# Scatters of a routed expert stage on GpSimd, with and without a small memset between them

## The chip, the cores and the metric

The kernel runs on one core of a Trainium2 chip. The metric is the device time of one execution in microseconds (us), median of several runs; lower is better. The engines are TensorE (PE in the profile), VectorE (DVE), ScalarE (ACT), GpSimd (POOL) and SyncE (SP). SP here only issues DMAs. POOL issues indirect DMAs, whose rows go to, or come from, places that a list of numbers names.

## What is computed

A small vision tower: 64 images become 4096 tokens of 256 numbers, then come an attention layer, a routed expert layer with 7 experts, a second attention layer and, last, a second expert layer. The change lies in that last layer. Cut to what matters, it is:

```
combine = _route(xf, router_weight, router_bias)      # top 4 of 16 experts, by groups
out = jnp.zeros_like(xf)
for e in range(E):                                    # E = 16
    g = xf @ w_gate[e].T
    u = xf @ w_up[e].T
    y_e = jax.nn.silu(g) * u @ w_down[e].T
    out = out + combine[:, e:e + 1] * y_e
```

Each token needs only 4 of the 16 experts, so the kernel sorts tokens by expert.

## The kernel before

The 4096 tokens lie in 32 blocks of 128 rows. `sorted_phase` (from line 1087, the last 400 us) takes them in three chunks and a dense rest: chunk 0 is blocks 0 to 7, chunk 1 blocks 8 to 19, chunk 2 blocks 24 to 31, and blocks 20 to 23 go through all 16 experts without sorting. For a sorted chunk:

1. PE computes router logits ("own" units), DVE picks the four experts of each token and works out where each row goes; the last step (L1493) writes `row_of` and releases POOL.
2. POOL scatters (L1254): for each block and each of its four choices one indirect DMA moves 128 normalised rows of 1 KB to the sorted list in HBM (`rows`; profile names leave the chunk out). That is 32 scatters for chunk 0, 48 for chunk 1, 32 for chunk 2. After every second one (`BURST` is 2) comes `rest()` (L1248): a memset of a small unused tile, the router bias of the first expert layer, and a wait until it has ended.
3. SP loads pairs of sorted blocks (`e_moved`, L1185, 256 KB each, four buffers). The first load of a chunk waits for all scatters of that chunk. PE turns the pair (L1592), multiplies it with the weights of its experts (L125), turns the hidden values (L1639) and multiplies again; ACT copies the result (`e_y`, L1322, two buffers), SP stores it (`results`, L1192). One such pair is called a unit. Chunk 0 has 24 units, chunk 1 32, chunk 2 24.
4. POOL gathers (L1273) the four results of each token, block by block, into a ring of three places, and DVE adds them to the residual `h` with their weights (`combine`, L1524: four instructions a block). The gathers of chunk 0 have a `rest()` after every second one, the later ones have none.

Each engine works through its program in order. POOL's is the tuple `MOVES`: scatter 0, 1, 2, then gather 0, 1, 2. DVE's `combine` of a block stands at a fixed unit of the stage, for chunk 0 every second unit from the 14th behind the chunk's end on (`combine1`). If the gathered rows are not there, DVE waits, and so do its steps for the units behind it, which PE needs. SP's queue is in order as well: while it waits for a chunk's scatters, the results behind it are not stored.

POOL's part of the stage begins at line 1224. The code of this stage follows.

Of the kernel before, what the change touches and what calls it, by code (L numbers as in the profile page):

```python
# [55 lines left out]
BURST = 2  # L56
# [1030 lines left out]
def sorted_phase(core, experts, chunks, dense, moves, combine_step, out):  # L1087
# [4 lines left out]
    top_k, at_member = TOP_K, experts // GROUPS  # L1092
# [7 lines left out]
    with ExitStack() as ctx:  # L1100
# [54 lines left out]
        def own_rows(n):  # L1155

            return core.xn0[:, n, :] if n < CH else xn[:, n - CH, :]

        def first_block(i):

            kind, c, j = flow.order[i]
            if kind == "dense":
                return flow.dense[c]
            return (dense if c == flow.dense_own else chunks[c])[0] + 2 * j
# [59 lines left out]
        @block.gpsimd  # L1224
        def _(pool):
            pool.memset(restart[:], 1.0)
            for part in restart_l:
                pool.memset(part[:], 1.0)
            pool.memset(ones[:], 1.0)
            for g in range(GROUPS):  # L1230
                pool.memset(wins[:, :, g:g + 1], float(g)).then_inc(consts, 1)
            pool.wait_ge(consts, GROUPS)
            pool.memset(restart[:, :, 0:1], 0.0)
            for part in restart_l:
                last = pool.memset(part[:, :, 0:1], 0.0)
            last.then_inc(consts, 1)
            for i in range(CH // 2, flow.front):
                n = first_block(i)
                for m in (n, n + 1):
                    last = pool.tensor_scalar(own_rows(m), core.h[:, m, :], core.mv[:, m, 0:1], core.rstd[:, m:m + 1],  # L1240
                                              ALU.subtract, ALU.mult)
                last.then_inc(xn_early, 1)

            cleared = Chain(pool, rested)

            def rest():

                cleared(pool.memset(idle[:], 0.0))  # L1248

            def scatter(c):  # L1250
                pool.wait_ge(routed, c + 1)
                for n in range(*chunks[c]):
                    for k in range(top_k):
                        pool.indirect_dma_start(out=d["rows"][c][0:rooms[c] * P],  # L1254
                                                out_offset=bass.IndirectOffsetOnAxis(ap=row_of[:, n, k:k + 1], axis=0),
                                                in_=own_rows(n), in_offset=None, bounds_check=rooms[c] * P - 1,
                                                oob_is_err=False).then_inc(scattered[c], 16)
                        if (n * top_k + k) % BURST == BURST - 1:
                            rest()

            def gather(c):
                if c == 0:
                    for sent in range(sum(low < CH + top_k * RING for low, _ in chunks)):
                        pool.wait_ge(scattered[sent], 16 * counts[sent] * top_k)
                for i in range(STORES):
                    pool.wait_ge(y_stored[i], 16 * sum(x % STORES == i for x in range(flow.moves_in[c])))
                for g, (of, n) in enumerate(entries):
                    if of != c:
                        continue
                    if g >= RING:  # L1270
                        pool.wait_ge(combined, g - RING + 1)
                    for k in range(top_k):
                        pool.indirect_dma_start(out=yg[g % RING][:, k, :], out_offset=None,  # L1273
                                                in_=d["results"][c][0:rooms[c] * P],
                                                in_offset=bass.IndirectOffsetOnAxis(ap=row_of[:, n, k:k + 1], axis=0),
                                                bounds_check=rooms[c] * P - 1, oob_is_err=False).then_inc(gathered[g % RING], 16)
                        if c == 0 and k % BURST == BURST - 1:
                            rest()

            for move, c in moves:  # L1280
                if move == "scatter":
                    scatter(c)
                else:
                    gather(c)
# [1527 lines left out]
```

## Time and profile before

| | |
|---|---|
| median of 3 runs | 1592.77 us (1591.8 to 1597.05) |
| time of the profiled execution | 1595.07 us |
| its span, first to last instruction | 1593.3 us |
| PE busy | 1388.4 us, 87% |
| DVE busy | 1046.1 us, 66% |
| POOL busy | 637.3 us, 40% |
| mean granted TensorE clock | 0.93 |

Times in the rows further down are us from the start of the span; those behind a line's instruction in square brackets are the idle time of the engine just before it, and what ended it. "issue" is a wait for nothing that the profile shows. A DMA instruction on POOL is busy while it writes the transfer's descriptors; the data move later. The scatters and gathers of the sorted stage run from 1222 us to 1584 us.

### The profile page before, as it was taken

The page shows a single profiled execution, that of the slowest core. Times are in us where ns is not written, and L with a number is a line of the kernel's source. Part 1 is how long each engine was busy: PE and PEld are TensorE (multiplying, and loading weights), DVE is VectorE, ACT ScalarE, POOL GpSimd, SP SyncE. Part 2 cuts the span into 40 slices and gives each one's busy share as a digit, 9 for nine tenths or more (in the row PEclk, how much of TensorE's full clock was granted, in tenths as well). Part 3 has the DMA queues.
Part 4 walks back from the last instruction along what each step waited for, and adds up shares of the span by engine and source line. Part 5 has one row for each costly group of instructions (what it writes and reads, how often), then busy time and mean ns, then how long its engine had stood idle before and what let it go on. Part 6 is the DMA issues. An engine that isn't in the chain of part 4 may idle for free. (4 is left out here: it accounts for less than half of the span.)

```text
span 1593.3 us, 37096 instructions
## 1 busy us (share of the span) xinstructions
PE 1388.4 (87%) x14188; PEld 1218.8 (76%) x14188; DVE 1046.1 (66%) x2196; ACT 759.9 (48%) x1288; POOL 637.3 (40%) x664
## 2 busy tenths in 40 slices
PE   6979999999999987868993788889976899999994
PEld 5867878888888876768992566667765889998994
DVE  4754574674674575776566577888858777556775
ACT  5424444444444443334552476678732355655641
POOL 4015322112112002535626264333445666663775
PEclk9999999999999998889997798999965999999997
DMA  7314754243354105135864010000026267887963
GB/s 286 119 29 149 236 192 146 90 158 123 107 163 145 43 2 199 66 107 184 247 198 127 6 31 25 1 2 2 2 92 248 84 200 244 257 257 235 287 212 112
DMA packets 142883, 215.57 MB, mean 135 GB/s; under 512 B 14336, under 2 KB 112768, under 8 KB 141824
## 3 DMA queue, kind: packets, MB, share of 16 engines
q1 hardware_dynamic: 121648, 160.20, 30.5%
q0 software_dynamic: 18624, 52.45, 10.3%
q8 instruction: 119, 1.95, 0.5%
q10 hardware_dynamic: 2448, 0.61, 0.2%
q14 instruction: 44, 0.36, 0.1%
HBM read 103.64 MB, written 109.58 MB: 134 GB/s over the span
## 5 line engine op out<-in xcount | busy, mean ns | idle before, releaser
L125 PE MATMUL e_p_gu<-e_w_hi,e_xt_hi 128*128 (+1 forms) x676 | 201.5, 298 | 12.1 <-DVE e_xt_lo L723 9.7
L125 PE MATMUL e_p_gu<-e_w_hi,e_xt_lo 128*128 (+1 forms) x676 | 195.7, 289 | 0.0
L125 PE MATMUL e_p_gu<-e_w_lo,e_xt_hi 128*128 (+1 forms) x676 | 195.5, 289 | 0.0
L125 PEld LDWEIGHTS e_p_gu<-e_w_hi,e_xt_hi 128*128 128x128 f32 x676 | 133.5, 197 | 14.3 <-issue 12.0
L1273 POOL DMA_INDIRECT e_xn<-results,e_row_of x112 | 115.3, 1030 | 63.1 <-issue 30.0
L125 PEld LDWEIGHTS e_p_gu<-e_w_lo,e_xt_hi 128*128 128x128 f32 x676 | 134.1, 198 | 0.0
L125 PEld LDWEIGHTS e_p_gu<-e_w_hi,e_xt_lo 128*128 128x128 f32 x676 | 134.0, 198 | 0.0
L125 PE MATMUL e_p_y<-e_w_hi,e_hid_hi 128*128 (+1 forms) x338 | 111.8, 331 | 7.3 <-DVE e_hid_lo L742 7.1
L1254 POOL DMA_INDIRECT rows<-e_xn,e_row_of x96 | 93.6, 975 | 56.6 <-POOL router_bias L1248 35.7
L1940 DVE TENSOR_TENSOR a_ot_lo<-a_O,a_ot_hi 128x1024 fp32r<-128x1024 f32 x32 | 39.1, 1223 | 114.6 <-ACT a_ot_hi L1883 114.6
L125 PE MATMUL a_J<-a_xt_hi,w_qk_hi 128*128 128x512 f32 x256 | 106.8, 417 | 7.9 <-DVE a_xt_lo L1958 5.9
L2223 POOL TENSOR_TENSOR a_s<-a_s,a_total 128x1024 f32<-128x1024 f32 x32 | 60.9, 1903 | 119.4 <-DVE a_total L2414 118.8
L125 PE MATMUL a_J<-a_xt_lo,w_qk_hi 128*128 128x512 f32 x256 | 101.3, 396 | 0.0
L125 PE MATMUL a_J<-a_xt_hi,w_qk_lo 128*128 128x512 f32 x256 | 101.2, 395 | 0.0
L1299 ACT ACTIVATE e_gated<-e_p_gu 128x256 f32<-128x256 f32 x112 | 43.1, 385 | 121.7 <-PE e_p_gu L125 121.7
L125 PE MATMUL e_p_y<-e_w_lo,e_hid_hi 128*128 (+1 forms) x338 | 96.9, 287 | 0.0
L125 PE MATMUL e_p_y<-e_w_hi,e_hid_lo 128*128 (+1 forms) x338 | 96.7, 286 | 0.0
L1357 DVE TENSOR_TENSOR e_xt_lo<-e_p_xt,e_xt_hi 128x512 fp32r<-128x512 f32 x98 | 67.5, 689 | 25.3 <-ACT e_xt_hi L1292 23.0
L1292 ACT CAST e_xt_hi<-e_p_xt 128x512 fp32r<-128x512 f32 x98 | 57.5, 587 | 50.9 <-PE e_p_xt L1592 47.0
L1837 POOL CAST w_qk_in<-w_qk_in 128x768 fp32r<-128x768 f32 x24 | 22.2, 924 | 146.2 <-DMA w_qk_in<-in_we 146.2
L125 PE MATMUL a_J<-a_w_hi,a_ot_hi 128*128 128x256 f32 x256 | 73.6, 287 | 7.7 <-DVE a_ot_lo L1940 7.6
L1856 POOL TENSOR_TENSOR h<-h,a_xn 128x1024 f32 x7 | 17.8, 2545 | 144.1 <-DVE a_xn L420 144.1
(335 smaller groups left out, 4408.7 us busy)
## 6 DMA issues: line engine op xcount, KB each, us to landing
e_moved<-rows SPq DMA_DIRECT2D x121, 256.0 KB, 3.9
results<-e_y SPq DMA_DIRECT2D x121, 256.0 KB
rows<-a_zero SPq DMA_DIRECT2D x28, 1024.0 KB, 5.8
pa_x<-in_x SPq DMA_DIRECT2D x7, 1536.0 KB, 6.5
w_qk_in<-in_we SPq DMA_DIRECT2D x24, 384.0 KB, 6.3
we_parts<-w_qk_in SPq DMA_DIRECT2D x24, 384.0 KB, 2.3
we_parts<-a_e_lo SPq DMA_DIRECT2D x24, 384.0 KB, 2.4
e_w_hi<-we_parts SPq DMA_DIRECT2D x4, 1536.0 KB, 16.2
```

The lines of the kernel that those rows point to most:

```text
L125: mm = eng.matmul(out, lhs[a], rhs[b], start=start and n == 0, stop=stop and n == len(terms) - 1, skip_group_check=skip)
L1254: pool.indirect_dma_start(out=d["rows"][c][0:rooms[c] * P], out_offset=bass.IndirectOffsetOnAxis(ap=row_of[:, n, k:k + 1], axis=0), in_=ow ...
L1273: pool.indirect_dma_start(out=yg[g % RING][:, k, :], out_offset=None, in_=d["results"][c][0:rooms[c] * P], in_offset=bass.IndirectOffsetOn ...
L1292: act.copy(xt[0][i % 2][:], p_xt[i % 2][:]).then_inc(xt_hi, 1)
L1299: act.activation(gated[h % 2][:], p_gu[h % 2][:].rearrange("p (b n) -> p b n", n=2 * INNER)[:, :, 0:INNER], ACT.Silu)\
L1357: dve.tensor_tensor(xt[1][i % 2][:], p_xt[i % 2][:], xt[0][i % 2][:].bitcast(F32), ALU.subtract).then_inc(xt_lo, 1)
L1837: pool.tensor_copy(e_hi, e_in).then_inc(e_split, 1)
L1856: pool.tensor_tensor(rows, rows, xn[:], ALU.add).then_inc(residual, 1)
L1940: dve.tensor_tensor(ot[1][:], p_o[:].rearrange("p i (j q) -> p j i q", q=SEQ), ot[0][:].bitcast(F32), ALU.subtract)\
L2223: pool.tensor_tensor(row_groups(s[c]), row_groups(s[c]), per_row(totals[c]), ALU.mult).then_inc(p_done, 1)
```

## The change

The pause behind every second scatter is gone in the second expert stage. The pauses between the gathers of chunk 0 stay (they are made by the same `rest()`), and so do all pauses of the first expert stage.

```diff
@@ -1255,8 +1255,6 @@
                                                 out_offset=bass.IndirectOffsetOnAxis(ap=row_of[:, n, k:k + 1], axis=0),
                                                 in_=own_rows(n), in_offset=None, bounds_check=rooms[c] * P - 1,
                                                 oob_is_err=False).then_inc(scattered[c], 16)
-                        if (n * top_k + k) % BURST == BURST - 1:
-                            rest()
```

POOL's program at the border between the scatters of chunk 1 (`rows1`) and of chunk 2 (`rows2`), before the change; `router_bias00` is the small tile that is cleared:

```order
L1254 DMA rows1<-e1_xn,e1_row_of 8192x256 x2
L1248 MEMSET router_bias00 128x8
L1254 DMA rows2<-e1_xn,e1_row_of 6144x256 x2
L1248 MEMSET router_bias00 128x8
L1254 DMA rows2<-e1_xn,e1_row_of 6144x256 x2
L1248 MEMSET router_bias00 128x8
```

POOL's program of the changed kernel, from the first scatter to the first gathers of chunk 0:

```order
L1254 DMA rows0<-xn0,e1_row_of 6144x256 x16
L1254 DMA rows0<-e1_xn,e1_row_of 6144x256 x16
L1254 DMA rows1<-e1_xn,e1_row_of 8192x256 x48
L1254 DMA rows2<-e1_xn,e1_row_of 6144x256 x32
L1271 DMA e1_xn<-results0,e1_row_of 128x256 x2
L1248 MEMSET router_bias00 128x8
L1271 DMA e1_xn<-results0,e1_row_of 128x256 x2
```

The 112 scatters now follow each other with nothing between them but the waits for `row_of` at a chunk's start; 56 memsets and 56 waits are gone. No other engine's program has changed.

## Rows read from the trace of the kernel before

**Rows 1.** The chain of waits, in order of time, around chunk 1's start.
```profile
1352.15 3.99 DMA rows<-e_xn,e_row_of
1356.15 2.78 DMA e_moved<-rows
1358.98 0.66 PE e_p_xt L1592 x4
1359.63 1.00 issue
```
**Rows 2.** Timeline of SP: results stored (start, us, instruction).
```profile
1351.43 0.36 SPq L1192 DMA_DIRECT2D results<-e_y  x1
...
1362.48 0.36 SPq L1192 DMA_DIRECT2D results<-e_y  x1
...
1410.10 0.36 SPq L1192 DMA_DIRECT2D results<-e_y  x1
...
1412.90 0.36 SPq L1192 DMA_DIRECT2D results<-e_y  x1
...
1456.32 0.36 SPq L1192 DMA_DIRECT2D results<-e_y  x1
```
**Rows 3.** Timeline of PE: the first turn of a sorted pair.
```profile
1276.75 1.37 PE L1592 MATMUL e_p_xt<-ident,e_moved 128*128 128x128 f32 x8 [0.99 <-DMA e_moved<-rows]
```
**Rows 4.** Timeline of DVE: combines of chunk 0 (first, sixth, last block).
```profile
1412.68 2.05 DVE L1524 SCALAR_TENSOR_TENSOR h<-e_xn,e_weight,h 128x256 f32<-128x256 f32 x4 [2.49 <-DMA e_xn<-results,e_row_of]
...
1448.18 2.05 DVE L1524 SCALAR_TENSOR_TENSOR h<-e_xn,e_weight,h 128x256 f32<-128x256 f32 x4 [3.61 <-DMA e_xn<-results,e_row_of]
...
1459.14 1.00 DVE L1524 SCALAR_TENSOR_TENSOR h<-e_xn,e_weight,h 128x256 f32<-128x256 f32 x2
```
**Rows 5.** Timeline of POOL: gathers of chunk 0, first of chunk 1.
```profile
1404.34 1.04 POOL L1273 DMA_INDIRECT e_xn<-results,e_row_of  x1 [0.80 <-POOL router_bias L1248]
...
1408.95 1.00 POOL L1273 DMA_INDIRECT e_xn<-results,e_row_of  x1 [0.30 <-issue]
...
1442.08 1.00 POOL L1273 DMA_INDIRECT e_xn<-results,e_row_of  x1 [0.30 <-issue]
...
1455.02 1.00 POOL L1273 DMA_INDIRECT e_xn<-results,e_row_of  x1 [0.30 <-issue]
...
1473.43 1.01 POOL L1273 DMA_INDIRECT e_xn<-results,e_row_of  x1 [17.29 <-DMA results<-e_y]
```
**Rows 6.** Timeline of POOL: chunk 1's first scatter; its end and chunk 2's first.
```profile
1277.96 0.97 POOL L1254 DMA_INDIRECT rows<-e_xn,e_row_of  x1 [5.24 <-DVE e_row_of L1493]
...
1350.88 0.97 POOL L1254 DMA_INDIRECT rows<-e_xn,e_row_of  x1 [0.78 <-POOL router_bias L1248]
1352.15 0.97 POOL L1254 DMA_INDIRECT rows<-e_xn,e_row_of  x1 [0.30 <-issue]
1353.11 0.13 POOL L1248 MEMSET router_bias<- 128x8 f32 x1
1354.02 0.97 POOL L1254 DMA_INDIRECT rows<-e_xn,e_row_of  x1 [0.78 <-POOL router_bias L1248]
```
**Rows 7.** Timeline of DVE: `row_of` of chunk 1 and of chunk 2.
```profile
1276.93 0.19 DVE L1493 TENSOR_SCALAR e_row_of<-e_top 128x48 int32<-128x48 f32 x1
...
1352.94 0.18 DVE L1493 TENSOR_SCALAR e_row_of<-e_top 128x32 int32<-128x32 f32 x1
```
**Rows 8.** Groups by line of POOL from 1473 to 1584: gathers without pauses.
```profile
L1273 POOL DMA_INDIRECT e_xn<-results,e_row_of x80 | 82.2, 1027 | 45.5 <-issue 24.0 <-DMA results<-e_y 17.6 <-DVE h L1524 3.9
```
**Rows 9.** Stretches: us, busy (count) of PE, PEld, DVE, ACT, POOL; PEclk, DMA share, GB/s.
```profile
1370.00:1404.00 34.00, 34.00 (x294) 34.00 (x293) 17.72 (x37) 22.34 (x50) 22.43 (x33) 1.00 0.87 271
...
1500.00:1520.00 20.00, 19.27 (x160) 18.53 (x159) 15.87 (x35) 12.38 (x27) 15.43 (x16) 1.00 0.97 301
```
**Rows 10.** DMA queues from 1370 to 1404: packets, MB, share of 16 engines.
```profile
q0 software_dynamic: 1041, 2.85, 24.1%
```
**Rows 11.** Timeline of ACT: a result copy that waited for a store.
```profile
1297.59 0.59 ACT L1322 COPY e_y<-e_p_y 128x512 f32<-128x512 f32 x1 [4.18 <-DMA results<-e_y]
```

## The prediction

> **What bounds the kernel now.** PE is the busiest engine, but the question is whether it ever stands still because of POOL. I went from the chain of waits to the timelines of the engines it names. There are three places in this stage where the scatters' pace reaches PE.
>
> First, chunk 1's start. The last scatter of chunk 1 lands, SP can load the first pair, and only then does PE turn it [rows 1]. PE passes one unit in 2.80 us when nothing holds it: results are stored at 1410.10 and 1412.90 [rows 2]. Between the result at 1351.43 and the one at 1362.48, the third after it, lie 11.05 us instead of 3 x 2.80 = 8.40. PE lost **2.65 us**, although four load buffers stood ahead of it.
>
> Second, chunk 0's start: PE waited 0.99 us for its first sorted pair [rows 3], which SP could load only when scatter 0 had landed. A loss of **0.99 us**.
>
> Third, and largest, the gathers of chunk 0. POOL comes to them at 1404.34, straight out of the last scatter [rows 5]. DVE stood ready for the first combine 2.49 us before its rows landed at 1412.68, and waited again later, last at 1448.18 for 3.61 us [rows 4]. DVE is in order, so PE's units slipped: from the result at 1412.90 to the twelfth after it at 1456.32 it is 43.42 us [rows 2] instead of 33.60. PE lost **9.82 us**. The combines slipped by as much: ready at 1412.68 - 2.49 = 1410.19 for the first block, and one block every second unit, the eighth would have begun at 1410.19 + 7 x 5.60 = 1449.39; it began at 1459.14 [rows 4], 9.75 late.
>
> After that POOL has 17.29 us in hand: its next gather waits for results of chunk 1 [rows 5], thus for PE. From there on PE's place in time sets everything, to the gathers at the end. So what PE wins before 1456 comes off the end, one for one, and nothing that POOL alone wins does.
>
> **The change part by part.** A pause costs 0.13 us of memset and 0.78 us of wait where two scatters otherwise stand 0.30 us apart [rows 6]: 0.91 - 0.30 = **0.61 us** for each. A scatter behind a scatter starts 1.27 us after it (1350.88 to 1352.15).
>
> *Scatter 0* has 15 pauses before its last scatter, 9.2 us. The wait of 0.99 us is gone, with 8 us to spare. Gain 0.99.
>
> *Scatter 1* starts when DVE has written `row_of` at 1276.93 [rows 7], which hangs on the dense units ahead, so it still starts near 1278. 48 scatters take 47 x 1.275 = 59.9 us to the last start, so that one starts at 1337.9 instead of 1352.15 [rows 6]: 14.2 us earlier. With the same 3.99 us to land [rows 1] the rows are there at 1341.9; SP asks for them at about 1351. Gain 2.65, whole, with 9 us to spare.
>
> *Scatter 2.* Here most of the lead is lost. POOL is done with chunk 1 at 1338.9, but `row_of` of chunk 2 is written at 1352.94 [rows 7]; before, POOL arrived just as it was written, so it did not show as a wait. A new wait of 13 us appears on POOL, and its only follower there is POOL itself. DVE reaches the place earlier only by the 0.99 us of PE. From the end of `row_of` to the first scatter it is 0.84 us (1277.12 to 1277.96). So scatter 2 starts at 1353.12 - 0.99 + 0.84 = 1352.97 instead of 1354.02 [rows 6], and the last of its 32 at 1352.97 + 31 x 1.275 = 1392.5. The first gather follows at 1393.8 instead of 1404.34: **10.5 us earlier**.
>
> *Gather 0* keeps its pauses. The last gathers of its eight blocks start between 1408.95 and 1455.02 [rows 5], 6.58 us apart, while DVE wants a block every 5.60 us. So POOL's lead melts by 1 us a block. Counting the 3.64 us that PE is already ahead, DVE is ready for block 1 at 1406.55, and its rows land by 1402.1 (8.34 us after the first gather as before): no wait. For block 8 it is ready at 1445.75. Its last gather starts at 1455.02 - 10.5 = 1444.5. From that start to the combine it was 3.73 us for block 1 and 6.10 for block 6 [rows 4, 5]; I take 4.1, since it makes block 8 fit its row before (1455.02 + 4.1 = 1459.1). Rows there at 1448.6, that is 2.9 us late. PE so loses 2.9 us instead of 9.8. Gain **6.9**. With 3.73 it is 7.3, with 6.10 it is 4.9.
>
> *Everything behind*: the wait of 17.29 us on POOL stays within a tenth as long, as both its sides move by the same amount. The memsets themselves hold up nobody else.
>
> The sum: 0.99 + 2.65 + 6.9 = **10.5 us**. Put otherwise, the chain of waits ran from `row_of` of chunk 2 along POOL to block 8, and it becomes 10.5 us shorter.
>
> *The unknown cost* is the pace of scatters in a long unbroken row, for which the trace has no case: never more than two. From below it is 1.27 us, as inside a pair; I see no reason for less, since the instruction's own 0.97 us is POOL's work. From above the nearest rows are gathers without pauses, 80 of them at 1.027 us each [rows 8] plus 0.30 between them, 1.33. That is 0.06 us more over 31 scatters, 1.8 us later. I take 1.275, a scatter being nearest to a scatter. The bounds so give gains of 6.7 (1.33 with 6.10 to land) to 10.9.
>
> **A rule against the change.** With the pauses gone the scatters come 1.57 / 1.275 = 1.23 times as often. From 1370 to 1404 the DMA engines were 0.87 busy at 271 GB/s [rows 9], of which POOL's queue had 24.1% [rows 10]; that becomes 29.7%, together 0.93. From 1500 to 1520, beside unpaused gathers, they are 0.97 busy at 301 GB/s and PE is busy 19.27 of 20 us. By this row the extra traffic costs nothing that PE feels. The Trainium skill's page "DMA: Bandwidth & Descriptors", section "SWDGE vs HWDGE vs iDMA", says that GpSimd's and SyncE's transfers sit in different queues of each DMA engine, between which it goes round in turn; by that, denser scatters take turns from SP's loads and stores. Taken by itself that rule would give the slower case below instead of a gain.
>
> **The rivals.**
>
> *Slower: stores fall behind.* The result tile has two buffers, so a store must land within two units, 5.60 us. One copy did wait 4.18 us for a store [rows 11], where DMA was thick and SP late. If the denser scatters lengthen the stores past that, ACT waits, and then PE in every unit that runs beside scatters: 61 + 40 = 101 us of them, 36 units. It decides from 10.5 / 36 = 0.29 us a unit on; at 0.4 us it costs 14.4 against 10.5, time **1597**. For it: 0.93 busy is a mean over engines and moments. Against: the stretch at 0.97. Chance 6%.
>
> *No change: the pauses were free.* If the DMA side, not POOL, set the pace of scatters, the wait would come back as a longer gap before each. Time **1592.8**. Against: the gap inside a pair is 0.30 us, and the gathers in long rows keep it too. Chance 8%.
>
> *Smaller: the gathers land later.* Gather 0 now runs beside units that are not slowed, so loads, stores and gathers meet more densely. If all blocks take 6.10 us or the pace is lower still, DVE waits most of what it did, and the gain is the 3.64 us of the two starts and about 2 to 3 more. Time **1587**. Chance 14%.
>
> *Larger: no late block at all.* DVE was busy for 17.72 of 34 us without combines [rows 9], and for some 4.9 of a unit pair's 5.60 with one, so a delay of 1 us can stay unseen by PE, and if the rows also land a little sooner none is seen. Then all 13.5 us come back. Time **1579.3**. Chance 14%.
>
> **How the numbers follow.** My case has 58%. The profiled execution took 1595.07 us, so it would take 1584.6; the runs' median is 2.3 us below it, thus 1592.8 - 10.5 = **1582.3 us**. The range reaches over the larger gain and most of the smaller one, to leave out no more than 2 in 10: 1578.5 to 1588.5. A measurement of this kernel tells about 0.3%, 4.8 us, from no change. My case, the larger one and nearly all of the smaller are beyond it: faster 0.84; within it the free pauses and a rest of the smaller case, 0.10; slower 0.06.
>
> **What the profile would show.** Scatters 1.27 us apart throughout. Chunk 1's last scatter near 1338, then an idle time of about 13 us on POOL ended by `row_of`. No PE wait for `e_moved` near 1276 and none near 1358. The first gather near 1394, DVE without a wait at block 1, and waits of together some 3 us at the last three blocks. POOL's wait before chunk 1's gathers still about 17 us, and the span 10 to 11 us shorter. The prediction is wrong if copies of `e_y` wait for stores again and again between 1290 and 1393, or if the gaps between scatters grow well past 0.30 us.

## The result, and the profile after

The changed kernel takes 1585.34 us (median of 6 runs, 1582.06 to 1588.56), the kernel before 1594.38 in the same comparison: 9.0 us less, ratio 0.9943, 95% interval 0.9925 to 0.9961. A second comparison (e9, below) gave 0.9929, 11.7 us by its medians. Forecast were 10.5 us.

Whole times of one and the same kernel lie up to 12 us apart here (the runs of the kernel before, in the comparison of e9: 1591.49 to 1603.41), so the traces are compared by a measure of their own, **the stage**: from the start of the first scatter of the second expert stage to the end of the span. Before it is 1593.3 - 1222.63 = 370.67 us, after it 1586.7 - 1228.09 = 358.61. That is 12.1 us less, while all that lies ahead of the stage, which the change does not touch, took 5.5 us more in the traced execution. For comparing places with [rows 1 to 7], take 5.46 us off the times of the changed kernel.

Timeline of POOL, changed kernel: first scatters of chunk 1, its last, first of chunk 2, first gather, first gather of chunk 1.

```profile
1283.51 0.97 POOL L1254 DMA_INDIRECT rows<-e_xn,e_row_of  x1 [13.89 <-DVE e_row_of L1491]
1284.79 1.97 POOL L1254 DMA_INDIRECT rows<-e_xn,e_row_of  x1 [0.30 <-issue]
...
1345.00 0.97 POOL L1254 DMA_INDIRECT rows<-e_xn,e_row_of  x1 [0.30 <-issue]
1356.29 0.97 POOL L1254 DMA_INDIRECT rows<-e_xn,e_row_of  x1 [10.31 <-DVE e_row_of L1491]
...
1397.54 1.04 POOL L1271 DMA_INDIRECT e_xn<-results,e_row_of  x1 [0.30 <-issue]
...
1466.13 1.01 POOL L1271 DMA_INDIRECT e_xn<-results,e_row_of  x1 [16.95 <-DMA results<-e_y]
```

Against [rows 6]: the 48 scatters of chunk 1 lie within 61.49 us, where it was 74.19. Most of that turns into the wait of 10.31 us for `row_of` of chunk 2. Against [rows 5]: the first gather comes 169.45 us into the stage instead of 181.71, 12.3 us earlier, and the wait before chunk 1's gathers is 16.95 us instead of 17.29, so from there on POOL has the same slack as before.

Timeline of DVE, changed kernel: combines of chunk 0 for blocks 1, 6, 7 and 8.

```profile
1410.51 2.04 DVE L1522 SCALAR_TENSOR_TENSOR h<-e_xn,e_weight,h 128x256 f32<-128x256 f32 x4
...
1438.80 2.08 DVE L1522 SCALAR_TENSOR_TENSOR h<-e_xn,e_weight,h 128x256 f32<-128x256 f32 x4
...
1446.14 2.05 DVE L1522 SCALAR_TENSOR_TENSOR h<-e_xn,e_weight,h 128x256 f32<-128x256 f32 x4 [1.22 <-DMA e_xn<-results,e_row_of]
...
1452.14 2.04 DVE L1522 SCALAR_TENSOR_TENSOR h<-e_xn,e_weight,h 128x256 f32<-128x256 f32 x4 [0.91 <-DMA e_xn<-results,e_row_of]
```

Against [rows 4]: no wait at the first six blocks, 2.13 us at the last two; before there were six waits of together 12.42 us.

Timeline of SP, changed kernel: the same results stored as in [rows 2], without the one at 1410.10.

```profile
1353.82 0.36 SPq L1192 DMA_DIRECT2D results<-e_y  x1
...
1362.22 0.36 SPq L1192 DMA_DIRECT2D results<-e_y  x1
...
1413.29 0.36 SPq L1192 DMA_DIRECT2D results<-e_y  x1
...
1448.33 0.36 SPq L1192 DMA_DIRECT2D results<-e_y  x1
```

Three units over chunk 1's start now take 8.40 us, exactly 3 x 2.80, where it was 11.05. The twelve units beside the gathers take 35.04 instead of 43.42.

The DMA engines while chunk 2 is scattered, changed kernel (us, busy of PE, PEld, DVE, ACT, POOL; PEclk, DMA share, GB/s):

```profile
1360.00:1396.00 36.00, 35.63 (x305) 35.37 (x304) 21.27 (x45) 23.44 (x52) 27.60 (x28) 1.00 0.93 290
```

The share is 0.93 at 290 GB/s, where it was 0.87 at 271 [rows 9], and PE is busy for 35.63 of 36 us. POOL's queue has 29.2% of the engines' time in this stretch; it was 24.1% [rows 10].

### The profile page after: what moved, and what is told of

It reads as the page before. It is cut to its first block and busy times, and to the rows that moved or that the text cites. A ratio compares the mean times of both kernels' runs of the same rounds, so it can differ in the third digit from the quotient of the medians.

```text
span 1586.7 us, 37038 instructions
## 1 busy us (share of the span) xinstructions
PE 1388.1 (87%) x14188; PEld 1219.2 (77%) x14188; DVE 1047.5 (66%) x2196; ACT 758.5 (48%) x1288; POOL 634.1 (40%) x608
## 3 DMA queue, kind: packets, MB, share of 16 engines
q0 software_dynamic: 18624, 52.45, 10.5%
## 5 line engine op out<-in xcount | busy, mean ns | idle before, releaser
L125 PE MATMUL e_p_gu<-e_w_hi,e_xt_hi 128*128 (+1 forms) x676 | 200.8, 297 | 12.9 <-DVE e_xt_lo L723 9.6
L1254 POOL DMA_INDIRECT rows<-e_xn,e_row_of x96 | 95.5, 995 | 52.9 <-issue 28.7
L625 POOL DMA_INDIRECT rows<-e_xn,e_row_of x56 | 54.6, 976 | 50.9 <-DVE e_row_of L812 22.2
```

The source lines that it names most:

```text
L125: mm = eng.matmul(out, lhs[a], rhs[b], start=start and n == 0, stop=stop and n == len(terms) - 1, skip_group_check=skip)
L625: pool.indirect_dma_start(out=d["rows0"][c][0:rooms[c] * P], out_offset=bass.IndirectOffsetOnAxis(ap=row_of[:, n, k:k + 1], axis=0), in_=o ...
L1254: pool.indirect_dma_start(out=d["rows"][c][0:rooms[c] * P], out_offset=bass.IndirectOffsetOnAxis(ap=row_of[:, n, k:k + 1], axis=0), in_=ow ...
```

## The experiments

Theory A is that of the prediction: what PE feels is POOL's time, at the starts of chunks 0 and 1 and, above all, along the chain from `row_of` of chunk 2 through its scatters to the gathers of chunk 0, which swallows what PE has won before. The main rival is that the gains of the three chunks stand apart and add up; another, that the DMA side and not POOL sets the pace. Each kernel is given with its stage by one trace, and the whole-time ratio to the kernel before of the same comparison.

| kernel | pauses left in the second stage | stage, us | against 370.66 | ratio, 95% interval |
|---|---|---|---|---|
| before, two traces | all | 370.67, 370.65 | | 0.9974 [0.9953, 0.9994] against itself |
| changed, two traces | gathers | 358.61, 357.45 | -12.1, -13.2 | 0.9943 [0.9925, 0.9961]; 0.9929 [0.9904, 0.9955] |
| e2 | chunks 0 and 1, gathers | 361.63 | -9.0 | 0.9930 [0.9908, 0.9952] |
| e3, e10 | chunk 2, gathers | 369.55, 370.48 | -1.1, -0.2 | 0.9949 [0.9928, 0.9970]; 1.0002 [0.9985, 1.0020] |
| e4, e12 | chunk 1, gathers | 365.90, 366.58 | -4.8, -4.1 | 0.9951 [0.9931, 0.9970]; 0.9964 [0.9946, 0.9982] |
| e5, e11 | all scatters, no gathers | 363.86, 366.55 | -6.8, -4.1 | 0.9994 [0.9971, 1.0017]; 0.9976 [0.9959, 0.9993] |
| e6 | none | 358.78 | -11.9 | 0.9932 [0.9907, 0.9957] |
| e7 | behind every scatter | 397.09 | +26.4 | 1.0182 [1.0151, 1.0213] |
| e8 | none, nor in the first stage | 357.73 | -12.9 | 0.9899 [0.9875, 0.9923] |

Read the first row first: the kernel against itself gives 0.9974, with an interval that leaves out 1. Whole-time ratios are thus good to some 0.5% and no better (e3 and e10 are one kernel, 0.9949 and 1.0002); the stage repeated to 0.02 us in the kernel before and to 0.7 to 2.7 us in four others.

**e1: the kernel before, again.**

> The kernel before, unchanged, for a second trace of it. Measure of the stage: span minus the start of the first scatter of the second expert stage, 1593.3 - 1222.6 = 370.7 us in the first trace. Theory A (the gain comes from POOL's time alone): 370 to 371.5 again, block 1's combine of chunk 0 waits about 2.5 us, and the eight together about 12.4 us. Theory B (1.5 us of the 12.1 us by which the changed kernel's stage was shorter were luck of TensorE's clock: before, the matmuls behind the wait for the counts of chunk 2 took 0.41 us instead of 0.28, after they did not): the slow matmuls at that place, near 1338, are missing here and the stage is about 369 us. If they are there again, they belong to the kernel before.

Measured: stage 370.65 us; block 1 waited 1.46 us and all eight together 14.73. The slow matmuls were an accident: the step behind this wait took 6.6 us in the first trace of the kernel before and 4.5 to 5.1 in the 13 others. Timeline of PE, first in the kernel before, then in e1, at the same place behind the wait for chunk 2's counts:

```profile
1338.98 0.41 PE L125 MATMUL e_p_gu<-e_w_lo,e_xt_hi 128*128 x1
```

```profile
1326.61 0.23 PE L1657 MATMUL e_p_small<-e_sel_bf,before_bf 128*128 128x128 bf16 x1 [1.64 <-DVE e_sel_bf L1442]
...
1327.14 0.28 PE L125 MATMUL e_p_gu<-e_w_hi,e_xt_lo 128*128 x1
```

The granted clock tells the two apart. Stretches of the kernel before and of e1 (columns as in [rows 9]):

```profile
1337.50:1340.00 2.50, 2.48 (x14) 2.40 (x15) 0.09 (x1) 0.00 (x0) 1.42 (x3) 0.64 0.93 288
```

```profile
1326.00:1330.00 4.00, 3.39 (x29) 3.31 (x30) 1.55 (x5) 1.34 (x4) 2.92 (x5) 1.00 0.74 231
```

It is 1.00, the 2.4 GHz level, all through the stretch of e1, and 0.64 as a mean in the other, where most matmuls ran at the 1.2 GHz level. The copies of `e_y` are 3.78 us later than in step at this place in the first trace and 2.09 in e1. But the stage did not become the 1.7 us shorter that I gave theory B. Timeline of PE in e1, the first pair of chunk 1:

```profile
1347.67 1.12 PE L1592 MATMUL e_p_xt<-ident,e_moved 128*128 128x128 f32 x4 [2.37 <-DMA e_moved<-rows]
```

PE came to this start 2.0 us earlier in the stage than in the first trace, waited 2.37 us there instead of 1.13, and left it at the lower clock (granted 0.55 from 1347 to 1352, where it was 1.00 behind the shorter wait of the first trace). So it came out 1.5 us later than in the first trace, not earlier. At the gathers it then lost less: the last block's combine begins 236.9 us into the stage, in the first trace 236.5. In sum, counted from copy to copy of `e_y` against 2.80 us, e1 lost 6.1 us at chunk 1's start and 8.4 at the gathers, the first trace 1.7 by the accident, 2.6 and 9.8. The single losses of PE differ, the end is POOL's, and that is what theory A says.

**e9: the changed kernel, again.**

> The changed kernel once more, for a second trace. In two traces of the kernel before, the stage (first scatter to end) was 370.67 and 370.65 us, while all that lies ahead of it took 1222.6 and 1212.1 us. Theory A (the stage's length is fixed by the chain on POOL and repeats; whole times differ because of what lies ahead): stage 358 to 360 us again (358.61 in the first trace), waits for the gathers of chunk 0 about 2 us. Rival (the stage itself varies by as much as the whole times): anything from 355 to 367.

Measured: stage 357.45 us, 1583.76 us against 1595.41, ratio 0.9929 [0.9904, 0.9955]. The waits at the eight combines are 0.86 + 0.22 = 1.08 us.

**e2: pauses removed in chunk 2 only.**

```diff
-                        if (n * top_k + k) % BURST == BURST - 1:
+                        if c in (0, 1) and (n * top_k + k) % BURST == BURST - 1:
```

> Pauses between scatters removed in chunk 2 only. Theory A (one chain on POOL, from row_of of chunk 2 through its scatters to the gathers of chunk 0, is what PE waits for at the end; the starts of chunks 0 and 1 are overtaken by it): the first gather comes 16 x 0.61 = 9.8 us earlier, the last block's rows land at 1449.3 on the old time line against DVE ready at 1449.4, so nothing is late and the gain is 9.4 to 9.8 us, nearly that of the whole change. Rival (the three gains stand apart and add): 6.9 us.

Measured: -9.0 us, and one wait of 0.22 us left at the eight combines. Not the 6.9 us of added gains. 16 of the 56 removed memsets bring 68 to 75% of what all bring (9.0 of 13.2 or 12.1 us).

**e3 and e10: pauses removed in chunks 0 and 1, kept in chunk 2.** The condition is `c in (2,) and ...`.

> Pauses removed in chunks 0 and 1, kept in chunk 2. Theory A: PE is 2.65 + 1 us earlier when chunk 0's gathers come, but these start only as much earlier as row_of of chunk 2 does, 1 us (up to 3 as measured in the changed kernel), so the combines wait longer than before (about 15 us in all instead of 12.4) and the gain is 1 to 3 us. Rival (gains add): 3.6 us or more, with the combines' waits unchanged at 12.4 us.

> Pauses kept in chunk 2 only, again: its stage was 1.1 us shorter than before by the trace, its whole times 8 us less by the medians, which do not fit. Theory A: stage 368 to 370.5 us again, combines waiting about 13 us, and the whole times' lead is from ahead of the stage (it should not repeat). Rival: the stage comes out 5 us or more shorter than 370.7.

Measured: -1.1 and -0.2 us. 40 of the 56 memsets are gone and next to nothing is won. Timeline of DVE in e3, the first combine of chunk 0:

```profile
1405.61 2.04 DVE L1524 SCALAR_TENSOR_TENSOR h<-e_xn,e_weight,h 128x256 f32<-128x256 f32 x4 [6.34 <-DMA e_xn<-results,e_row_of]
```

It waited 6.34 us (6.55 in e10), where before it was 2.49 and 1.46. Both starts are clean in these traces, PE has no wait for a first pair, and the lead is given back whole at the gathers, which start 179.4 us into the stage, 2.3 and 3.1 us earlier than in the two traces of before. The waits of the eight together came to 13.28 and 14.26 us. The whole-time gain of e3 (8 us) did not come back in e10 (ratio 1.0002). By e3's trace it lay ahead of the stage, which began at 1216.85 us; for the runs without a trace that is not shown.

**e4 and e12: pauses kept in chunk 1 alone.** The condition is `c in (1,) and ...`.

> Pauses kept in chunk 1 alone, removed in chunks 0 and 2. Theory A: the start of chunk 1 still costs PE 2.65 us, but this was time that the gathers' lateness would take anyway: block 8 is ready for DVE at 1448.4, its rows are there at 1448.6; gain 10.4 us, the same as with the whole change (its own runs: 9 us) within 1 us. Rival (gains add): 2.65 us less than the whole change.

> Pauses kept in chunk 1 alone, again. Its stage was 365.9 us; of the 10.4 us expected, 4.8 came. In the trace chunk 1's scatters took 76.2 us instead of 74.2 and PE, waiting 6.4 us for the first pair, came out of it at the lower clock for another 1.1 us. If both belong to this kernel (a scatter of 1.97 us near the start of chunk 1 stands in every kernel in which chunk 0 is free), the stage is 365 to 366.5 us again. If they were chance, it is 361 to 363 us: PE leaves chunk 1's start where it did before, no later, and gains the 9.8 us of the gathers.

Measured: -4.8 and -4.1 us, where I expected 10.4. This was my miss. No combine waits here (0 us in both), so the gathers are not at fault. The loss is at chunk 1's start. Timeline of PE in e4:

```profile
1358.63 1.11 PE L1592 MATMUL e_p_xt<-ident,e_moved 128*128 128x128 f32 x4 [6.40 <-DMA e_moved<-rows]
```

I had set the cost of this start at the 2.65 us of before. But chunk 1's rows come at a time of their own, fixed by `row_of` of chunk 1 and 48 scatters; PE, which came to it 4.0 us (e4) and 2.1 us (e12) earlier than in the first trace of before, has to give that back too, so this start takes PE's lead to nothing. In addition the 48 scatters took 76.23 and 75.32 us instead of 74.19, so that the last one started 1 to 2 us later; single scatters of 1.56 to 1.97 us account for it (see the last section). And behind waits of 6.40 and 3.77 us the turns took 1.11 and 1.12 us instead of 0.66 [rows 1], at the lower clock (granted 0.50 from 1358.6 to 1362 in e4), which the next unit shows as another 1.1 and 0.9 us. Counting from the stage's start, the 23rd copy of `e_y` lies at 144.9 and 146.3 us in the two traces of before, at 144.7 in e2, at 148.2 and 147.1 here, and at 139.1 and 139.8 with the change. So chunk 1 alone, on top of chunks 0 and 2, brings 7.3 us (365.90 - 358.61; in the second traces 9.1), though chunks 0 and 1 together, without chunk 2, bring at most 1.1.

**e5 and e11: pauses between scatters kept, those between chunk 0's gathers gone.**

```diff
-                        if c == 0 and k % BURST == BURST - 1:
-                            rest()
```

> The kernel before with all pauses between scatters, but without the 16 between the gathers of chunk 0. Theory A: the gathers start at 1404.3 as before, DVE waits 2.5 us for block 1, and then POOL takes 4 x 1.31 = 5.24 us a block against 5.60 that DVE wants, so the lateness no longer grows: PE loses 2.5 us instead of 9.8, gain 7.3 us. Rival (the landing of the gathers, not POOL's pace, is what is late, and denser gathers only land later): gain under 3 us.

> Pauses between the gathers of chunk 0 removed, those between scatters kept, again: stage 363.86 us by its trace (6.8 less than before), whole times by the medians as before. Theory A: stage 363 to 365 us again, and the medians this time below the kernel before. Rival (the trace caught a lucky execution): stage near 370 us.

Measured: -6.8 and -4.1 us, with 3.77 and 3.49 us of waits left, all but 0.54 of them at the first two blocks. The gathers' lateness no longer grows, as expected, so POOL's pace was the matter and not the landing. The gain is 0.5 to 3.2 us short of the 7.3 expected. The medians of whole times (0.9994, 0.9976) say less than the traces do; both profiled executions were the fastest of their 12 runs.

**e6: no pause in the second stage.**

> The changed kernel, and the 16 pauses between the gathers of chunk 0 gone too. Theory A: the changed kernel had waits of 1.22 and 0.91 us left at blocks 7 and 8; with 5.24 us a block POOL stays ahead and they vanish, so 1.5 to 2.5 us less than the changed kernel, 11 to 13 us less than before. Rival (the DMA side is full, and it is that which made them wait): the same time as the changed kernel or more, with more and longer waits for e_moved and for stores of e_y.

Measured: -11.9 us. The last waits of the combines are gone (0 us), but the stage is no shorter than with the change (358.61, 357.45). Of what I had expected in addition nothing came. The trace shows small losses of PE instead, beside the gathers: 0.73, 1.35, 0.90 and 0.70 us. Timelines of SP and of PE in e6, at the second of them:

```profile
1423.38 1.55 SPq L1198 DMA_DIRECT2D out_h<-h  x1
1424.97 0.48 SPq L1185 DMA_DIRECT2D e_moved<-rows  x1
```

```profile
1429.60 0.66 PE L1588 MATMUL e_p_xt<-ident,e_moved 128*128 128x128 f32 x4 [0.15 <-DMA e_moved<-rows]
1430.95 0.41 PE L1635 MATMUL e_p_ht<-ident,e_gated 128*128 128x128 f32 x2 [0.70 <-DVE e_gated L1370]
```

SP took 1.55 us to issue one store of `out_h` instead of the usual 0.47, and the load behind it, issued at 1424.97, was the one that the turn at 1429.60 needed, 4.6 us later. The same stands in the changed kernel, in its chain of waits (start, duration, engine or DMA):

```profile
1436.32 1.60 SPq L1198
...
1437.96 4.58 DMA e_moved<-rows
...
1442.58 0.66 PE e_p_xt L1590 x4
```

Loads stand behind the stores of results in SP's order, so here a load is issued about 4.6 us before its turn, some 1.6 units of 2.80 us, and not by the four buffers' 11 us; a landing takes as long, and a slow issue of SP reaches PE. The denser scatters and gathers are not shown to be the cause: issues of 1.1 to 2.4 us by SP stand in the sorted part of all 14 traces, those of the kernel before too (in e1 of 1.46, 1.16 and 1.29 us between 180 and 220 us into the stage). Why they are slow stays open.

**e7: a pause behind every scatter.** The condition in front of `rest()` is taken away.

> The kernel before with a pause behind every scatter instead of every second: 56 more, 0.61 us each. Theory A: chunk 0's rows come 16 x 0.61 = 9.8 us later, all of it a wait of PE; chunk 1's last scatter 20 us later, of which PE feels about 10 more; the gathers start 30 us later. In all slower by 28 to 32 us, near 1623 us. Rival (the scatters' pace is hidden behind PE except for the wait of the gathers): slower by 9.8 us.

Measured: stage +26.4 us where 28 to 32 were expected, whole times 1622.33 against 1595.69, ratio 1.0182. Timelines of PE and DVE in e7, the starts of chunk 0 and 1 and the first combine:

```profile
1282.44 1.97 PE L1591 MATMUL e_p_xt<-ident,e_moved 128*128 128x128 f32 x8 [11.50 <-DMA e_moved<-rows]
...
1372.83 1.11 PE L1591 MATMUL e_p_xt<-ident,e_moved 128*128 128x128 f32 x4 [8.11 <-DMA e_moved<-rows]
```

```profile
1436.35 2.05 DVE L1523 SCALAR_TENSOR_TENSOR h<-e_xn,e_weight,h 128x256 f32<-128x256 f32 x4 [10.84 <-DMA e_xn<-results,e_row_of]
```

All three places wait, for 11.50, 8.11 and 10.84 us. A rival in which only the gathers count (9.8 us) is out. The first gather is 210.84 us into the stage, 29 us later.

**e8: no pause in either expert stage.** The four lines are gone from `shared_phase` too.

> No pause in either expert stage. In the first stage the pauses stand behind every second of 64 scatters and behind every second block's gathers of its chunk 0. Theory A gives no number for the first stage before its trace is read; there POOL waits for row_of (21.7 us in the groups by line) and for results (27 us), so most of the lead is lost: expected gain over the kernel without pauses in the second stage 0 to 4 us. Rival: a loss, if denser scatters disturb that stage's loads.

Measured: 1578.03 us against 1595.69 in the same comparison, ratio 0.9899 [0.9875, 0.9923], the fastest kernel of this study. The stage is 357.73 us. From the first scatter of the first expert stage (653.84) to that of the second (1217.07) are 563.2 us, where it was 571.5 and 566.1 in the two traces of before and 576.0 and 570.9 in those of the changed kernel. So the first stage brings some 3 to 13 us more by the traces. By the medians of the same comparison it is 6.8 us (e6 takes 1584.8 us), within a noise of about as much.

## Why the prediction was right, point by point

**What bounds.** Right. The three places were the ones at which PE got its time back, and e7 made all three wait longer.

**Scatter 0, 0.99 us.** The wait is gone. With the change the first copy of `e_y` is 0.5 us earlier in the stage, the fifth 1.6 us; the term came out between 0.5 and 1.6 us, by the trace and the copy taken.

**Scatter 1, 2.65 us.** At the place 11.05 became 8.40, right to the hundredth, but the size was luck: in e1, the same kernel, this start cost 6.1 us. The new wait for `row_of` of chunk 2 is there, 10.3 us instead of 13, because DVE wrote it earlier than reckoned. Timeline of DVE, changed kernel:

```profile
1355.33 0.18 DVE L1491 TENSOR_SCALAR e_row_of<-e_top 128x32 int32<-128x32 f32 x1
```

**Scatter 2, first gather 10.5 us earlier.** It was 12.3 us (169.45 against 181.71; 170.15 in the second trace). The step that was off is the time of `row_of`: I took it from a trace in which PE had run slow for two units just before (e1) and moved it by 0.99 us. The slow units cost the kernel before nothing, as its POOL reached chunk 2 only at 131.4 us anyway; in the changed kernel POOL stands and waits, and there they would count. `row_of` was finished at 130.49 us before, 128.56 in e1, 127.42 and 128.11 with the change.

**Gather 0, 6.9 us.** From the results stored it was 43.42 - 35.04 = 8.4 us. DVE's waits left were 2.13 us (1.08 in the second trace) instead of 2.9, with the same cause. They cost PE even less: of the 1.44 us above 33.60 that these twelve units took, 1.20 were lost at the unit whose load SP issued late (see e6), and behind DVE's waits of 1.22 and 0.91 us two later results are stored 0.34 and 0.36 us late. So the gathers still cost about 0.7 us, not 2.9. The 4.1 us from block 8's last gather to its combine had been fitted to a block that did not wait in the trace of before, so it bounded the landing only from above; with the change, where block 8 did wait, it was 4.33 and 4.24 us, and the choice did no harm.

**The loads' cover.** Thinner than stated: four load buffers stood in the sum, SP's order leaves about 4.6 us (e6). It cost 1.20 us at one unit of the changed kernel and 1.35 at one of e6.

**The pace of scatters.** Taken as 1.275 us, measured 39.97 / 31 = 1.289 in chunk 2 and 61.49 / 47 = 1.308 in chunk 1 (1.287 without one scatter of 1.97 us), between the bounds of 1.27 and 1.33.

**The sum.** 10.5 us forecast; the stage is 12.1 and 13.2 us shorter, whole times 9.0 and 11.7. The terms belong to one trace: e1 lost 6.1 and 8.4 us where the prediction read 2.65 and 9.82, and another 1.7 us of the first trace were the accident, which is in no term. The sum held better than its terms because its other reading, the chain on POOL from `row_of` of chunk 2 to block 8, is what set the end.

**The rivals.** Stores never fell behind: the copy that waited for a store did so for 4.12 us after, 4.18 before [rows 11], at the same unit, and nowhere else in the scatters' stretches. The DMA share came out at the 0.93 that was worked out from the rows, and the share of POOL's queue at 29.2% against 29.7. The pauses were not free: the gaps between scatters stayed at 0.30 us without them. By the rule of the Trainium skill's page "DMA: Bandwidth & Descriptors" (section "SWDGE vs HWDGE vs iDMA") the denser scatters take turns from SP's transfers; the trace neither shows nor excludes the turns, but from 1360 to 1396, at 290 GB/s, it shows no unit that became longer for it, bar one by 0.65 us.

**What I had wrong** is the interplay, and it shows only in parts of the change. I took the starts' costs as fixed sums. They are meeting points: PE's lead at chunk 1's start is whatever it brings less what the rows' own time allows. The forecast for the whole change did not depend on it, since every chain was shortened together.

## What to carry to other kernels

When several chains meet one engine in turn, the gain of shortening one is cut off at the next meeting point that still runs at its old time: here 40 of 56 removed waits brought at most 1.1 us while the last chain was left, and all brought 12 to 13 us. Cost such a change by the time at which each meeting point becomes free, not by adding stalls; and look in the trace of before at what the waiting engine would be ready for if it came earlier, since a value that was late without harm becomes the new bound. Where whole times of one kernel scatter by 12 us, measure from a fixed event inside the trace to the end.

## What had not been expected of the hardware

Two things. In all eight traces in which chunk 0's scatters have no pauses, the second scatter of chunk 1 takes 1.96 or 1.97 us instead of 0.97. Timeline of DVE, changed kernel, at that moment:

```profile
1284.70 1.20 DVE L1497 TENSOR_TENSOR e_work<-e_cum,steps 1x1024 f32<-1x1024 f32 x1
```

DVE reads two operands from SBUF on one partition for 1.20 us from 1284.70 on; the scatter starts 0.09 us behind it, at 1284.79, and ends 0.86 us after its end, about as long as it takes alone. The same instruction falls otherwise in other runs. Timelines of DVE and POOL, the kernel before (its second scatter of chunk 1), then e2 (its third):

```profile
1279.72 1.20 DVE L1499 TENSOR_TENSOR e_work<-e_cum,steps 1x1024 f32<-1x1024 f32 x1
1279.23 0.97 POOL L1254 DMA_INDIRECT rows<-e_xn,e_row_of  x1 [0.31 <-issue]
```

```profile
1281.80 1.20 DVE L1499 TENSOR_TENSOR e_work<-e_cum,steps 1x1024 f32<-1x1024 f32 x1
1282.21 1.64 POOL L1254 DMA_INDIRECT rows<-e_xn,e_row_of  x1 [0.78 <-POOL router_bias L1248]
```

A scatter that starts 0.49 us ahead of the operation takes its 0.97 us; one that starts 0.41 us behind it takes 1.64 us and again ends 0.85 us after it. This holds throughout: all 23 scatters of this stage above 1.25 us, in the 14 traces, started 0.09 to 0.41 us behind the start of a VectorE operation with two operands in SBUF and ended 0.84 to 0.87 us after its end. Beside operations with an operand in PSUM (`e_xt_lo<-e_p_xt,e_xt_hi`, over 200 times) none took more than 0.98. The Trainium skill's page "SBUF — State Buffer", section "SBUF: two separate sides", says that an operation of VectorE with two SBUF inputs and one of GpSimd that reads SBUF shut each other out for the whole instruction. The rows agree with it where VectorE comes first. Where the scatter comes first they do not: VectorE's operation takes 1.20 us then too.

The other is the spread ahead of the stage: the first scatter starts between 1212.1 and 1228.1 us in thirteen traces whose programs are the same up to there. What varies there was not looked into.
